# The place of an up tile's store in the sync queue, and of eight u loads, in a cross-attention and quantized FFN kernel

## What is computed

```python
x = x + attention(layernorm(x), ctx, Wq, Wkv)
h = act_qdq(layernorm(x))
up = act_qdq(h @ lpbq_dequant(w_up).T)
gate = act_qdq(h @ lpbq_dequant(w_gate).T)
gate = act_qdq(gate * fixed_qdq_u16(sigmoid(gate)))
out = x + act_qdq(gate * up) @ lpbq_dequant(w_down).T
```

## Time and profile before

| what | us |
|---|---|
| median of 3 runs | 917.21 (916.35 to 920.21) |
| the profiled execution's own time | 921.58 |
| its span, first to last instruction | 919.8 |
| PE busy | 877.8 (95%) |
| DVE busy | 660.0 (72%) |
| ACT busy | 567.4 (62%) |
| PE L867, up product, x1152 | 251.0 busy, 7.6 idle before |
| ACT L957, copies out of PSUM, x194 | 153.8 busy |

### The profile page before, as it was taken

One profiled execution on the slowest core, in us unless ns is written; L12 is line 12 of the kernel. 1 busy time (PEld: TensorE's weight loads), 2 busy tenths in 40 slices (PEclk: granted clock), 3 DMA queues, 4 the chain that ended last, 5 costly groups with the idle time before them and its releaser, 6 DMA issues.

```text
span 919.8 us, 12151 instructions
## 1 busy us (share of the span) xinstructions
PE 877.8 (95%) x4308; PEld 441.2 (48%) x4308; DVE 660.0 (72%) x954; ACT 567.4 (62%) x693; POOL 145.8 (16%) x109
## 2 busy tenths in 40 slices
PE   7999889999999999999999969999499989999998
PEld 5788664444444444444444424444144434444443
DVE  4999886732346243279986769847599998899892
ACT  2479877543553455399986769843489975545430
POOL 0199940076002910000000000000000000000000
PEclk9999999999999999999999999999799999999999
DMA  9722216434369559973448993799988787989872
GB/s 344 319 93 93 114 71 248 163 138 171 137 236 291 205 180 303 325 274 138 161 158 321 327 336 139 269 362 320 395 305 267 272 312 260 403 301 389 323 282 108
DMA packets 92319, 226.57 MB, mean 246 GB/s; under 512 B 31984, under 2 KB 31984, under 8 KB 90096
## 3 DMA queue, kind: packets, MB, share of 16 engines
q1 hardware_dynamic: 91120, 221.80, 66.9%
q10 hardware_dynamic: 1152, 4.19, 1.2%
HBM read 127.40 MB, written 92.27 MB: 239 GB/s over the span
## 4 chain that ended last, share of the span: by engine, by line
PE 69%; DVE 12%; DMA 8%; issue 5%; ACT 3%; SPq 2%; POOL 0%; DVEq 0%; ACTq 0%
PE ps L834 27%; PE ps L867 18%; PE ps L912 13%; PE ps L939 3%; DVE big L1540 3%; DVE big L1533 3%; DMA up_park<-big 3%; PE ps L707 3%; DMA big<-gate_park 2%; DMA big<-in_L_ffn_w_gate_dram 2%; PE ps L768 2%; PE ps L785 2%; PE ps L929 1%; ACT big L957 1%; DVE big L1304 1%
## 5 line engine op out<-in xcount | busy, mean ns | idle before, releaser
L957 ACT ACTIVATE big<-ps 128x1024 f32<-128x1024 f32 (+2 forms) x194 | 153.8, 813 | 208.6 <-PE ps L834 104.6
L867 PE MATMUL ps<-big 128*128 (+1 forms) x1152 | 251.0, 381 | 7.6 <-ACT big L957 7.6
L834 PE MATMUL ps<-big 128*128 (+1 forms) x1152 | 248.8, 379 | 0.5 <-DVE big L1410 0.5
L867 PEld LDWEIGHTS ps<-big 128*128 128x128 f16 x1152 | 112.9, 98 | 145.6 <-issue 7.0
L834 PEld LDWEIGHTS ps<-big 128*128 128x128 f16 x1152 | 112.6, 98 | 136.5 <-DVE big L1410 0.8
L1428 DVE TENSOR_REDUCE small<-big 128x1 f32<-128x1024 f32 (+1 forms) x48 | 58.4, 1219 | 135.8 <-ACT big L957 135.7
L912 PE MATMUL ps<-big 128*128 128x512 f16 x576 | 125.1, 379 | 2.6 <-DVE big L1561 2.6
L893 PE MATMUL ps<-big 128*128 128x512 f16 x384 | 86.3, 388 | 11.5 <-DMA big<-wdown_park 11.0
L912 PEld LDWEIGHTS ps<-big 128*128 128x128 f16 x576 | 56.2, 98 | 71.1 <-issue 3.6
L648 POOL PARTITION_ALL_REDUCE small<-small x9 | 3.6, 411 | 542.4 <-DVE small L1507 186.8
L1478 DVE CUSTOM_DVE_ANT_0 big<-big,small 128x1024 f32<-128x1024 int16 x48 | 61.7, 1285 | 7.0 <-DVE small L1472 0.2
(11 more groups left out here) (103 smaller groups left out, 1007.5 us busy)
## 6 DMA issues: line engine op xcount, KB each, us to landing
big<-up_park SPq DMA_DIRECT2D x90, 512.0 KB, 5.8
up_park<-big SPq DMA_DIRECT2D x48, 512.0 KB, 4.6
gate_park<-big SPq DMA_DIRECT2D x42, 512.0 KB, 2.7
big<-gate_park SPq DMA_DIRECT2D x42, 512.0 KB, 6.3
sign_park<-big SPq DMA_DIRECT2D x48, 256.0 KB, 2.2
big<-in_x_dram SPq DMA_DIRECT2D x8, 1024.0 KB, 18.0
x_park<-big SPq DMA_DIRECT2D x8, 1024.0 KB, 3.9
product_park<-big SPq DMA_DIRECT2D x16, 512.0 KB, 4.1
```

The lines of the kernel that those rows point to most:

```text
L834: mm = nc.tensor.matmul(ps[:, 2 * (n % 2) + j], w[:, a, k, o:o + P], XT[:, g, b, k], start=(k == 0 and a + b == 0), stop=(k == KC - 1 and ...
L867: mm = nc.tensor.matmul(ps[:, b + j], WU[:, a, k, o:o + P], XT[:, g, c, k], start=(k == 0 and a + c == 0), stop=(k == KC - 1 and c == 1))
L957: return nc.scalar.activation(dst, src, ACT.Copy)
```

## The change

Two edits, both in the order of the SP queue alone; no instruction of the other engines and no transfer is added or removed.

In steps 1 to 31 of the first stage, `park_up(n - 1)` is issued at the head of step n, behind `first_gates(n)`, ahead of the step's product stores and refills. Before, it was issued behind the first product store of the step and the refill that goes with it.

In the second stage, the three waits and the first four of the eight `EARLY` loads stand ahead of `park_up(43)` (n = `B_UNIT` + 10), the other four ahead of `park_up(44)` (n = `B_UNIT` + 11), each behind the sign loads of its step. Before, all eight stood ahead of `park_up(45)`.

```diff
--- before.py
+++ after.py
@@ -495,13 +495,13 @@
             for n in range(A_UNITS):
                 if n < 30:
                     first_gates(n)
+                if n:
+                    park_up(n - 1)
                 for i in steps(n):
                     if KEPT <= i < KEPT + PARKED:
                         park_product(i)
                     if KEPT < i <= KEPT + PARKED:
                         refill(i - 1)
-                    if n and i == steps(n)[0]:
-                        park_up(n - 1)
                 if n == 30:
                     first_gates(n)
             park_up(A_UNITS - 1)
@@ -520,11 +520,14 @@
                 if n > B_UNIT:
                     for t in range(signs_given(n - 1) + 4 if n > B_UNIT + 1 else 0, min(signs_given(n) + 4, NS)):
                         fetch_sgn(t)
-                if n == B_UNIT + 12:
+                if n == B_UNIT + 10:
                     sp.wait_ge(bact_d, NU // 2)
                     sp.wait_ge(bdve_d, NU // 2)
                     sp.wait_ge(u_mm, 7 * UPG)
-                    for c in EARLY:
+                    for c in EARLY[:4]:
+                        fetch_up_c(c)
+                if n == B_UNIT + 11:
+                    for c in EARLY[4:]:
                         fetch_up_c(c)
                 park_up(n)
```

## The result

| | before | after |
|---|---|---|
| median | 918.45 us (916.35 to 920.21, 5 runs) | 913.33 us (911.04 to 914.32, 5 runs) |
| ratio | | 0.9943, 95% interval 0.9927 to 0.9960 |
| the profiled execution | 921.58 us | 914.32 us |

0.9943 of 918.45 is 5.2 us less; the interval allows 3.7 to 6.7.

What follows compares the result with a forecast made beforehand. Late issue of up stores was taken to delay ScalarE's copies and so TensorE, with gate tiles late next. Terms of 6.0 and 1.2 us, 7.2 us off 917.21, gave 910.0 us, range 905.0 to 915.5.

Steps and rivals of the forecast that it cites:

- What bounds the kernel: Up product: stores issued late hold ScalarE 19.0 us, its copies come late; gaps and clock cost TensorE 9.7 us.
- The first term: First stage: up stores issued sooner let gate 39 land 6.0 us sooner, and the stage moves with it.
- the 0.95 I had set: Sign of the first step: DMA share from 471.5 to gate 39's landing rises from 0.90 to 0.95 or more.
- a gap of 1.9 us and no fall of the clock: Up product, ahead of unit 30: the gap left to TensorE, too short for the clock to fall.
- The second term: End of the up product: u loads in two lots fill free DMA time between 635 and 645, gaining 1.2 us.
- The argument that bytes ahead of store 46 stay the same: Second stage: the queue works in order of issue, so store 46 gains only the free time, 1.2 us.
- All from 658.46 on moves as a whole: From the first u product on: same work in the same order, so the 7.2 us gain carries through.
- The cover of the sign chain: Second stage: ScalarE's first u pass ends at 655.8, before store 46 lands at 657.3, a cover of 1.5 us.
- DMA was the bound all along: Rival, before gate 39: the gain is handed to the refills, gate 39 gains 1 to 3 us; 914.5 us, chance 0.27.
- my case: The forecast for the whole kernel: gain of 4.6 to 9 us, 908 to 912.6 us, chance 0.47.
- That gates would be late by more than the stores gained: Rival, first stage: gate 39 lands 6 us later, kernel slower by 4.8 us, 922.0 us, chance 0.07.
- The full gain: Rival: queue kept full near 387 GB/s, gate 39 gains 8 to 12 us; 907.0 us, chance 0.19.

Runs made afterwards that it cites:

- e2: The second edit alone (u loads in two lots) against the kernel before: ratio 0.9995, 917.6 us.
- e1: The first edit alone (up store ahead of the step's products and refills) against the kernel before: ratio 0.9950, 914.9 us.
- e6: Both edits, but all eight u loads ahead of store 43: ratio 0.9980 against before, 917.6 us.
- e8: Both edits plus eleven small idle matmuls in TensorE's gap ahead of the down product: 916.7 us in one execution.
- e5: The kernel before, unchanged, profiled a second time: 915.7 us in one execution.
- e10: Both edits, unchanged, profiled a second time: 915.8 us in one execution.
- e9: Both edits, with first gates of bench slots 4 to 7 one step sooner and parked products moved only by their first half: 905.1 us in one execution.
- e4: Both edits, with the 16 parked products stored and loaded only by their first half: 905.2 us in one execution.
- e3: Both edits, with the first gates of bench slots 4 to 7 loaded one step sooner: ratio 0.9910 against before, 910.6 us.

## Why the prediction was right, and where not

I predicted 910.0 us and a gain of 7.2 us; the median is 913.33 and the gain 5.2 us. Of the 3.3 us between, 1.2 are the base: the median of before is 918.45 over five runs, not 917.21. The time lies in the range of 905.0 to 915.5.

**What bounds the kernel.** Right. The store waits were the lateness of issue, and they went when the issue came sooner. That the gate would be late next, and would set the size of the gain, was right too: the wait for gate 39 is 6.8 us in after.

**The first term, 6.0 us.** Mechanism right, size half as much again too large. Gate 39 landed 5.1 us sooner in the first pair of traces (538.0 against 543.1), and the settle 5.1 us sooner, 5.4 when measured from the start of the up product. That pair flatters the edit. Three profiles without it (before, its second, e2) have the settle at 190.5 to 191.4 us, five with it and nothing else changed in the first stage (after, its second, e1, e6, e8) at 186.0 to 188.3: the means are 190.9 and 187.0, 3.9 us apart. e1 alone gives 0.5% in time, 4.6 us, with an interval of 2.7 to 6.4.

The step that was mis-sized is the share of free DMA time that gets filled: of 7.2 us I took 6.0. The DMA share rose from 0.90 to 0.94, under the 0.95 I had set. The free time fell from 7.2 to 4.0 us, so 3.2 were filled, and another 2.2 us came from the 1.1 MB fewer in the stretch, about half of them the store of tile 14, which now goes out ahead of it. In the second pair (e5, e10; from the first product store to gate 39) the shares are 0.92 and 0.93, and the free time fell from 5.6 to 4.7 us, by 0.9. SP now stands longer on the landing of a product store before a refill, which grew from 11.0 us to 24.3, while its waits for products fell from 49.2 to 25.3:

```profile
SPq L465 <- DVE small L1481: 25.3, 10, 4.9
SPq L417 <- DMA product_park<-big: 24.3, 11, 6.4
```

That this is what keeps the queue from filling is read from the waits; no run tests it alone.

**TensorE.** I had a gap of 1.9 us and no fall of the clock; in after it was 2.53 us and none, and TensorE ended 251.5 us after its start, not 258.6: 7.1 us sooner, against 7.3 forecast. That was luck. In the four other profiles with the first edit (e1, e6, e8, e10) the one gap is 3.39 to 4.89 us, the clock falls to 0.50 behind it, and TensorE ends after 255.1 to 256.4 us, where the second profile of before has 255.6. That TensorE would gain more than the stage after it can use, and that the first u product follows the settle, was right for these kernels.

**The second term, 1.2 us.** Not borne out. The timed runs alone can't exclude it (0.9995, 0.9978 to 1.0011: a gain of up to 2.0 us). The traces show nothing of it: from the settle to the first u product it is 77.2 us with the second edit alone and 77.3 in the second profile of before, 77.3 twice with both edits and 76.6 with the first alone. The failing step is the free time, read from one execution: 0.88 in its stretch, 1.01 in the second profile of the same kernel. The argument that bytes ahead of store 46 stay the same, so that only free time counts, fits this.

**All from 658.46 on moves as a whole.** Nearly. From the first u product to the start of the down product it is 91.7 us in all four profiles of the two kernels, but from there to the end both profiles of both edits had 1.3 us more, the slow matmuls, by a clock that I had not looked at.

**The cover of the sign chain.** Forecast 1.5 us. In after the first u pass ended at 647.69 + 1.14 = 648.8 and the store landed for 649.96: 1.1 us. In e8, the same kernel up to there, it was gone without any edit: the first u product was released by ScalarE's u pass. e6 used it up, and the first u product came later by what was left over.

**The rivals.** That DMA was the bound all along is more than half true. Its case had gate 39 gain 1 to 3 us; between the three profiles without the first edit and the five with it, it is 3.7 us, nearer to that than to my 6.0. The timed gain of 5.2 us lies in my case (4.6 to 9), and its interval (3.7 to 6.7) reaches into this rival's 1.5 to 4.2. The gain went partly to waits for gates (7.8 of 14.3 us). That the time came out near the forecast, with one term half too large and the other at nothing, is in part luck. That gates would be late by more than the stores gained did not come: it would have needed 14.3 us, and it was 7.8. The full gain did not come because the gate waits rose.

**Issue time and rate.** e1 brought 4.6 us by a change of order, more than the two issues of 0.4 us that a store is spared, since SP's time here is waiting on semaphores. In DMA: Bandwidth & Descriptors, section Issuing engines are not separate DMA queues, the Trainium skill says that starting DMAs on several engines at once saves only the sequencer's time to start them; that is about the engines that issue, and no rule on the order within one queue.

At the end of the up product of after, where u stores and weight loads follow one another, the DMA moved 418 GB/s; in the stretch before gate 39, where products, stores and refills alternate, 331 GB/s at a share of 0.94, which is 352 GB/s at full share. So the waits in the queue are not all of the difference; what makes the rest stays open. The Trainium skill, HBM Reference, section Specifications (TRN2), has about 425 GB/s for a core that streams alone: the trace comes near it in the first of these stretches and not in the second.

```profile
640.00:650.00 10.00, 3.76 (x24) 3.79 (x24) 6.96 (x13) 2.31 (x3) 0.35 (x1) 0.66 1.03 418
```

## What to carry to other kernels

In a queue that one engine issues in program order, the question is for each transfer how long it stood ready before it was issued, and what stands ready behind it: moving the one that releases the slowest engine first pays until the transfers pushed back release something later, and then the two waits must be weighed together (here stores against gates: 19.0 + 4.1 us became 4.7 + 11.9). Where the queue is full, the order of need decides and not the order of readiness: loads that nobody needs yet, ahead of a store that everybody waits for, cost 6.6 us at the end of this up product (the first u product 11.8 us behind the last up matmul, and 5.2 with the new order). Once TensorE ran without a gap, a stage that ended sooner beside it gained nothing (e9 against e4). A free share of DMA read from one execution is no term of a sum; a second profile of the kernel before would have removed it.

## What the runs showed of the hardware

The same code had DMA-bound stages of different length: from the settle to the first u product 80.8 us in one profile of before and 77.3 in the other, with 76.6 to 78.1 in six more profiles of kernels with the same bytes there (after, e1, e2, e3, e8, e10).

The clock behind a gap of TensorE in the up product: after gaps of 2.20, 1.04, 2.53, 2.92, 2.31 and 0.58 us the matmuls went on at full speed (432 in 93.41 us where they follow as one run, granted clock 1.00). After 2.75 us (e5) and 2.76 us (e2) they did not: the granted clock was 0.50 in the first 2.5 us, and 48 matmuls took 11.96 and 11.90 us where 48 x 0.2161 = 10.4 are due.

```profile
532.92 11.96 PE L867 MATMUL ps<-big 128*128 x48 [2.75 <-ACT big L957]
```

After 3.39, 3.52, 3.67, 4.35 and 4.89 us 432 matmuls took 96.13, 96.28, 96.01, 95.10 and 95.97 us, with the clock at 0.50 to 0.66 of full in the first 5 us (the lower level, 1.2 GHz, for all or most of them). The second profile of both edits:

```profile
545.00:550.00 5.00, 3.52 (x9) 1.33 (x10) 4.71 (x9) 4.91 (x6) 0.00 (x0) 0.50 0.52 204
550.00:555.00 5.00, 5.00 (x21) 2.08 (x20) 4.86 (x8) 4.82 (x5) 0.00 (x0) 0.82 0.26 105
```

So these gaps cost 1.7 to 2.9 us more than themselves, and those of 2.75 and 2.76 us about 1.5. The length of the gap alone does not decide: 2.92 us had none of it and 2.75 had, and ahead of the down product a gap of 2.40 or 2.41 us brings slow matmuls in five profiles (clock 0.66 to 0.70 in the first 5 us) and none in six (1.00).
